# Layer 2's scan over both halves at once, with a prepared seam; drives made in pairs; thirteen of 32 states weighed on GpSimd

## The chip, the core and the metric

One core of a Trainium2 chip runs the whole program; the other cores are idle. The metric is the device time of one execution in microseconds (us). The kernel before took 38,971.14 us (median of three runs, 38,961.69 to 39,000.97).

## The reference, cut to what matters

Sixteen images of 64 x 64 pixels and 128 channels go through four layers, each of which normalises its input over the image and adds its result to it: linear attention, a Fourier layer, and two selective-scan layers (a cross scan in four directions over 256 channels with 16 states, then a plain one over 128 channels with 8 states). The change lies in the third of them, numbered 2. The reference's step of such a scan is, here in the form of layer 3:

```python
def step(h, inp):
    d_t, u_t, b_t, c_t = inp
    dA = jnp.exp(d_t[..., None] * A)
    h = dA * h + (d_t * u_t)[..., None] * b_t[:, None, :]
    y_t = jnp.einsum('bdn,bn->bd', h, c_t)
    return (h, y_t)
```

d_t is a softplus, dA the decay, d_t * u_t * b_t the drive, and the product with c_t the weighing.

## The kernel before

The outer loop takes one image after another. Layer 2's 256 channels stand as two halves of 128 partitions side by side, 512 pixels each, so a tile is 128 x 1024. A unit is one state of one chunk of 512 pixels: 4 directions x 8 chunks x 16 states make 512 units an image. g counts chunks over all directions, c chunks in a direction, n states, k directions; from k = 2 on the scan runs backwards. For each unit u:

- SyncE copies the rows of B and C to all partitions by DMA, two states at a time, four buffers deep (spread_rows, line 423).
- GpSimd multiplies du = softplus x input by the row of B into one of six tiles Q: make_drive (line 543, instruction at line 550), three units ahead.
- ScalarE writes the decays of the two halves to PSUM, one exponential for each (decays, line 1202), one unit ahead. The banks alternate between even and odd units.
- VectorE scans each half with tensor_tensor_scan (states, line 1585, instruction at line 1598). The first chunk starts from 0.0, later ones from the column that the chunk before left in HST2.
- ScalarE's carry (line 1219) copies the last column of the scan to HST2. It comes after the decays of u+1 in ScalarE's queue.
- The product with the row of C is made by VectorE (weigh, line 1606) or, for six of the 16 states, by GpSimd (weigh, line 554, instruction at line 561), which waits for the carry, since it overwrites the tile that the carry reads.
- TensorE adds the product up over the states with an identity matrix, and after the 16th VectorE takes the sum to SBUF (take_y, line 1568).

Each engine works through its queue in order, and the loops over u in the scan2 of each engine write this order out by hand. Between the units, chunk g+1 is prepared: TensorE's rows2 and steps2 (lines 830 and 839), ScalarE's split2 and softplus2 (1157 and 1165), VectorE's log_small2 (1556), then GpSimd's sum_dt (528) for each half and make_du (535). All ScalarE instructions are issued at line 1050, all matmuls but the transposes at line 668.

Layer 3 does the same with one half, 8 states and 64 units (block3 of each engine; project, variance and project_out at lines 981 to 994; VectorE's take_y, fuse and add at 1683, 1705 and 1715). At the end of an image SyncE stores it, loads the next (lines 497 to 506), waits for the four engines, clears every semaphore of the image (line 509) and lets them go on (meet, line 514). VectorE then takes the statistics of the new image (line 1448).

## Time and profile before

| | us |
|---|---|
| median of three runs | 38,971.14 |
| the profiled execution's own time | 38,973.72 |
| its span, first to last instruction | 38,971.8 |
| TensorE busy | 28,928.2 (74%) |
| VectorE busy | 33,856.0 (87%) |
| ScalarE busy | 20,211.0 (52%) |
| GpSimd busy | 30,997.3 (80%) |
| image one: layers 0 and 1, and layer 2 up to its scan | 0 to 331 |
| image one: scan of layer 2 | 331 to 2130 |
| image one: rest of layer 2, and layer 3 | 2130 to 2454 |

PE is TensorE's matmuls, PEld its weight loads, DVE VectorE, ACT ScalarE, POOL GpSimd and SPq SyncE's queue. In a row of a timeline stand the start in us, the duration in us, engine, line, operation, what is written and read, and the number of instructions merged; in brackets the idle time of the engine just before, and who ended it. PS is PSUM, WORK, XN and BIG are SBUF regions (Q, DT and half of the C rows lie in WORK, the B rows in XN). Instructions that follow each other closely overlap by some hundredths of a microsecond, so the distance from start to start is a little less than the duration.

### The profile page before, as it was taken

The page shows a single profiled execution, that of the slowest core. Times are in us where ns is not written, and L with a number is a line of the kernel's source. Part 1 is how long each engine was busy: PE and PEld are TensorE (multiplying, and loading weights), DVE is VectorE, ACT ScalarE, POOL GpSimd, SP SyncE. Part 2 cuts the span into 40 slices and gives each one's busy share as a digit, 9 for nine tenths or more (in the row PEclk, how much of TensorE's full clock was granted, in tenths as well). Part 3 has the DMA queues.
Part 4 walks back from the last instruction along what each step waited for, and adds up shares of the span by engine and source line. Part 5 has one row for each costly group of instructions (what it writes and reads, how often), then busy time and mean ns, then how long its engine had stood idle before and what let it go on. Part 6 is the DMA issues. An engine that isn't in the chain of part 4 may idle for free. (4 is left out here: it accounts for less than half of the span.)

```text
span 38971.8 us, 271091 instructions
## 1 busy us (share of the span) xinstructions
PE 28928.2 (74%) x61540; PEld 11465.7 (29%) x61540; DVE 33856.0 (87%) x33741; ACT 20211.0 (52%) x38037; POOL 30997.3 (80%) x14776
## 2 busy tenths in 40 slices
PE   7777777777777777777777777777777777777777
PEld 3232232322323223232232322323223232232322
DVE  8979889798897988979889798897988979889798
ACT  4545545455454554545545455454554545545455
POOL 6949869498694986949869498694986949869497
PEclk8898888988888888898888988888898898888988
DMA  3424334243342433424334243342433424334243
GB/s 114 151 95 151 137 111 151 96 152 135 112 151 96 152 134 111 151 96 151 136 112 151 95 152 134 111 151 95 152 136 112 152 96 152 134 113 151 96 152 134
DMA packets 1387318, 5029.11 MB, mean 129 GB/s; under 512 B 164272, under 2 KB 165816, under 8 KB 1381440
## 3 DMA queue, kind: packets, MB, share of 16 engines
q1 hardware_dynamic: 1385536, 5010.20, 37.0%
q8 instruction: 526, 8.62, 0.1%
q14 instruction: 1256, 10.29, 0.1%
HBM read 4938.25 MB, written 71.30 MB: 129 GB/s over the span
## 5 line engine op out<-in xcount | busy, mean ns | idle before, releaser
L668 PE MATMUL PS<-WORK,CST 128*128 128x512 f32 x36096 | 19719.3, 690 | 8147.0 <-POOL WORK L561 7315.7
L550 POOL TENSOR_TENSOR WORK<-WORK,XN 128x1024 f32<-128x1024 f32 x8192 | 19311.4, 2395 | 324.6 <-ACT BIG L1050 324.6
L668 PEld LDWEIGHTS PS<-WORK,CST 128*128 128x128 f32 x36096 | 7495.5, 219 | 20640.2 <-POOL WORK L561 10104.7
L1050 ACT ACTIVATE PS<-WORK,AN 128x512 f32<-128x512 f32 x17408 | 11306.4, 679 | 1828.1 <-DVE WORK L1606 1024.8
L1598 DVE TENSOR_TENSOR_SCAN PS<-PS,HST,WORK 128x512 f32<-128x512 f32 x8960 | 10971.9, 1271 | 29.7 <-ACT PS L1050 16.1
L1598 DVE TENSOR_TENSOR_SCAN WORK<-PS,HST,WORK 128x512 f32<-128x512 f32 x5376 | 6583.5, 1267 | 0.0
L561 POOL TENSOR_TENSOR WORK<-WORK,CWIDE 128x1024 f32<-128x1024 f32 x2048 | 4888.4, 2387 | 117.4 <-issue 59.7
L1050 ACT ACTIVATE HST<-PS 128x2 f32<-128x2 f32 x5152 | 859.0, 167 | 6498.6 <-DVE WORK L1606 6063.0
L1606 DVE TENSOR_TENSOR WORK<-PS,WORK 128x1024 f32<-128x1024 f32 x3072 | 3762.1, 1225 | 105.1
L638 POOL MEMSET XN<- 128x66 f32 x32 | 4.9, 154 | 4158.8 <-DVE SM L1452 4036.2
L1050 ACT ACTIVATE WORK<-PS,DTB 128x512 f32<-128x512 f32 x2304 | 1555.8, 675 | 2103.9 <-DVE WORK L1563 1669.6
L1050 ACT ACTIVATE WORK<-PS 40x512 f32<-40x512 f32 (+2 forms) x1600 | 933.8, 598 | 3163.2 <-PE PS L668 2859.3
L1606 DVE TENSOR_TENSOR WORK<-PS,CWIDE 128x1024 f32<-128x1024 f32 x2048 | 2508.3, 1225 | 69.9
L561 POOL TENSOR_TENSOR WORK<-WORK 128x1024 f32<-128x1024 f32 x1024 | 2450.9, 2393 | 25.5 <-DVE WORK L1598 23.1
L668 PE MATMUL PS<-XN,TAP 128*128 128x512 f32 x4608 | 2058.9, 601 | 34.6 <-DVE XN L1468 34.6
L533 POOL TENSOR_TENSOR WORK<-WORK 128x512 f32<-128x512 f32 x1024 | 1338.6, 1307 | 808.2 <-DVE WORK L1563 808.2
L607 POOL TENSOR_TENSOR WORK<-WORK 128x512 f32<-128x512 f32 x1024 | 1276.4, 1271 | 836.7 <-DMA WORK<-xbc_rows 769.0
L668 PE MATMUL PS<-BIG,XP 128*40 128x512 f32 x2304 | 1667.8, 810 | 293.9 <-ACT BIG L1050 293.9
L1050 ACT ACTIVATE WORK<-WORK,VEC 128x512 f32<-128x512 f32 x2304 | 1631.3, 708 | 0.0
L1598 DVE TENSOR_TENSOR_SCAN PS<-PS,WORK 128x512 f32<-128x512 f32 x1280 | 1489.7, 1209 | 121.9 <-ACT PS L1050 121.9
L540 POOL TENSOR_TENSOR WORK<-WORK,BIG 128x1024 f32<-128x1024 f32 x512 | 1354.8, 2646 | 1.3
L668 PE MATMUL PS<-WORK,DTW 8*128 8x512 f32 x2304 | 1286.5, 639 | 0.0
(161 smaller groups left out, 24604.0 us busy)
## 6 DMA issues: line engine op xcount, KB each, us to landing
XN<-xbc_rows SPq DMA_DIRECT2D x4096, 512.0 KB, 3.7
WORK<-xbc_rows SPq DMA_DIRECT2D x2816, 512.0 KB, 4.3
CWIDE<-xbc_rows SPq DMA_DIRECT2D x2304, 512.0 KB, 4.2
BIG<-in_spec_dram SPq DMA_DIRECT2D x32, 2048.0 KB, 12.1
X<-in_x_dram SPq DMA_DIRECT2D x68, 512.0 KB, 4.7
xbc_rows<-WORK SPq DMA_DIRECT2D x512, 64.0 KB, 3.1
out_dram<-X SPq DMA_DIRECT2D x64, 512.0 KB, 5.1
xbc_rows<-WORK SPq DMA_DIRECT2D x128, 32.0 KB, 1.6
```

The lines of the kernel that those rows point to most:

```text
L533: nc.gpsimd.tensor_tensor(dt, dt, S.LE[:, ch(h)], ADD).then_inc(S.dt_made, 1)
L540: nc.gpsimd.tensor_tensor(S.like(S.DU[g % 2], g), S.like(S.DT[g % 2], g), S.cols(BIG1, g), MUL).then_inc(S.du_ready, 1)
L550: nc.gpsimd.tensor_tensor(S.both(S.Q[u % 6]), S.both(S.DU[u // SN % 2]), S.wide(S.BW, u).unsqueeze(1).to_broadcast([P, 2, NT]), MUL).then_ ...
L561: nc.gpsimd.tensor_tensor(q, q, S.wide(S.CW, u).unsqueeze(1).to_broadcast([P, 2, NT]), MUL).then_inc(S.weighed_pool, 1)
L607: nc.gpsimd.tensor_tensor(S.Q[u % 6], S.DU[u // SN3 % 2], S.wide(S.BW, u), MUL).then_inc(S.drive, 1)
L638: nc.gpsimd.memset(XN3[:, 0, :], 0.0).then_inc(frame_zero, 1)
L668: return nc.tensor.matmul(o, w, r, start=start, stop=stop)
L1050: return nc.scalar.activation(o, i, f, **k)
L1598: r = V.tensor_tensor_scan(o, a, b, HST2[:, 2 * n + h:2 * n + h + 1] if c else 0.0, MUL, ADD)
L1606: V.tensor_tensor(S.both(S.Q[u % 6]), PS[:, lo:lo + 2, :], S.wide(S.CW, u).unsqueeze(1).to_broadcast([P, 2, NT]), MUL).then_inc(S.weighed_ ...
```

## The change

- **Scan.** states makes one scan over 1024 columns, through two neighbouring PSUM banks. So that the second half does not go on from the first, ScalarE's prepare(g) overwrites one column of DT, at the seam, with 1e33: the decay there becomes 0. What the second half starts from is put in the drive: seam(u) adds HST2 x decay to that one column of Q, by a ScalarE instruction on one element per partition whose scale and bias are both read by pointer. prepare(g) first takes the true decays of that column for all 16 states (AT2). The first chunk of a direction has no seam.
- **ScalarE's queue** at unit u is: decays of u+1, a part of the preparation of a later chunk, seam of u+2, carry of u. seam(u+2) waits for the drive of u+2 and for the carry of the chunk before.
- **Drives.** GpSimd makes the drives of u+2 and u+3 in one instruction of 2048 columns, at even u; both semaphore counts come at its end. It waits for the sums up to unit u-3. Its weighing of u comes behind it.
- **Weighing.** Of 32 units in a row, thirteen are weighed on GpSimd: 1, 3, 6, 8, 11, 13, 17, 19, 22, 24, 26, 28, 30.
- **Softplus.** The sum of its two parts is made by TensorE in PSUM (sum_dt2) and copied out by ScalarE (copy_dt2) instead of by GpSimd. The rows and steps of a chunk are made one chunk earlier.
- **Layer 3.** The last chunk's project, variance and project_out go to banks 3 and 4 instead of 7 and 5 and are spread over the states of the last round; the loops end one round earlier.
- **Between images.** 33 semaphores of layers 0 and 1 are cleared by SyncE inside spread_rows (i = 16), 39 of layer 2 inside spread_rows3 (i = 12). The statistics of the next image's first four chunks are taken before the engines meet.

The core of the diff:

```diff
@@ -24,7 +24,7 @@
 POOL_STATES3 = (2, 5)
-POOL_STATES = (1, 4, 6, 9, 12, 14)
+POOL_STATES = (1, 3, 6, 8, 11, 13, 17, 19, 22, 24, 26, 28, 30)
...
@@ -288,7 +302,7 @@
-                return u % SN in s.pool
+                return u % (2 * SN) in s.pool
...
@@ -311,6 +325,19 @@
+            def seam(s, k):
+                return (NT, 1) if k < 2 else (NT - 1, 0)
+            def long(s, u):
+                lo = s.banks(u)[0]
+                return PS[:, lo:lo + 2, :].rearrange("p b l -> p (b l)")
+            def prepares(s, g):
+                return sum(2 if v % NCH else 1 for v in range(g + 1))
...
@@ -318,6 +345,11 @@
+            def two(s, u):
+                at = 2 * NT * (u % 6)
+                return WORK[:, at:at + 4 * NT].rearrange("p (n d l) -> p n d l", n=2, d=2)
...
@@ -438,6 +470,9 @@
                             e.wait_ge(S.rows_stored, 16 * (i // 8 + 1))
+                        if i == 16:
+                            for t in past_layer1:
+                                e.sem_clear(t)
                         if i >= 4:
...
@@ -467,6 +512,9 @@
                             e.wait_ge(S.rows_stored, 16 * (i // 4 + 1))
+                        if i == 12:
+                            for t in past_layer2:
+                                e.sem_clear(t)
                         if i >= 4:
...
@@ -497,7 +546,8 @@
-                    e.sem_clear(x_loaded[i])
+                    if i >= 2:
+                        e.sem_clear(x_loaded[i])
...
@@ -505,10 +555,11 @@
                 e.wait_ge(sample_done, 4)
-                for s in persistent + [sample_done]:
-                    e.sem_clear(s)
+                for s in persistent + x_loaded[0:2] + [sample_done]:
+                    if s not in past_layer1 and s not in past_layer2:
+                        e.sem_clear(s)
                 e.sem_inc(next_sample, 1)
-            for i in range(4):
+            for i in (2, 3):
                 e.wait_ge(x_loaded[i], 16)
...
@@ -518,19 +569,14 @@
+            nc.gpsimd.memset(LIM[:, 0:1], 1e33).then_inc(lim_set, 1)
+            nc.gpsimd.memset(LIM[:, 1:2], -1e-30).then_inc(lim_set, 1)
...
-                def sum_dt(g, h):
-                    e.wait_ge(S.dt_steps, 4 * g + 2 * h + 2)
-                    e.wait_ge(S.softplus, 12 * g + 6 * h + 6)
-                    dt = S.DT[g % 2][:, ch(h)]
-                    nc.gpsimd.tensor_tensor(dt, dt, S.LE[:, ch(h)], ADD).then_inc(S.dt_made, 1)
...
@@ -540,16 +586,16 @@
-                def make_drive(u):
+                def make_drives(u):
...
-                        e.wait_ge(S.summed, u - 5)
-                    nc.gpsimd.tensor_tensor(S.both(S.Q[u % 6]), S.both(S.DU[u // SN % 2]),
-                                            S.wide(S.BW, u).unsqueeze(1).to_broadcast([P, 2, NT]),
-                                            MUL).then_inc(S.drive, 1)
+                        e.wait_ge(S.summed, u - 4)
+                    rows = S.BW[u // 2 % 4].rearrange("p (n l) -> p n l", n=2)
+                    nc.gpsimd.tensor_tensor(S.two(u), S.both(S.DU[u // SN % 2]).unsqueeze(1).to_broadcast([P, 2, 2, NT]),
+                                            rows.unsqueeze(2).to_broadcast([P, 2, 2, NT]), MUL).then_inc(S.drive, 2)
...
@@ -561,23 +607,15 @@
-                sum_dt(0, 0)
-                sum_dt(0, 1)
...
-                for u in range(3):
-                    make_drive(u)
+                make_drives(0)
...
-                    if g + 1 < KDIR * NCH:
-                        if n == 8:
-                            sum_dt(g + 1, 0)
-                        if n == 11:
-                            sum_dt(g + 1, 1)
-                        if n == 12:
-                            make_du(g + 1)
-                    if u + 3 < S.units:
-                        make_drive(u + 3)
+                    if g + 1 < KDIR * NCH and n == 12:
+                        make_du(g + 1)
+                    if u % 2 == 0 and u + 2 < S.units:
+                        make_drives(u + 2)
...
@@ -829,26 +867,35 @@
-                if h == 0 and g:
-                    e.wait_ge(S2.dt_steps, 4 * g)
+                if g:
+                    e.wait_ge(S2.dt_made, 2 * g - 1)
...
-                o = S2.like(bank(6), g)[0:40, 0]
+                o = S2.like(bank(7), g)[0:40, 0]
...
+                if g:
+                    e.wait_ge(S2.dt_made, 2 * g)
...
+            def sum_dt2(g, h):
+                e.wait_ge(S2.softplus, 12 * g + 6 * h + 6)
+                e.wait_ge(S2.dt_steps, 4 * g + 2 * h + 2)
+                mm(bank(7 - h), EYE, S2.DT[g % 2][:, ch(h)], True, False)
+                mm(bank(7 - h), EYE, S2.LE[:, ch(h)], False, True).then_inc(S2.dt_summed, 1)
...
-                        e.wait_ge(S.dt_steps, 4 * KDIR * NCH)
+                        e.wait_ge(S.dt_made, 2 * KDIR * NCH)
...
@@ -857,12 +904,19 @@
-                        if n < 2:
-                            rows2(g + 1, n)
-                        if n in (3, 4):
-                            steps2(g + 1, n - 3)
+                        if n == 5:
+                            sum_dt2(g + 1, 0)
+                        if n == 8:
+                            sum_dt2(g + 1, 1)
...
+                    if g + 2 < KDIR * NCH:
+                        if n == 9:
+                            for h in range(2):
+                                rows2(g + 2, h)
+                        if n == 12:
+                            for h in range(2):
+                                steps2(g + 2, h)
...
@@ -895,6 +949,17 @@
+                    if j == 4:
+                        for h in range(2):
+                            sum_dt2(0, h)
+                    if j == 5:
+                        e.wait_ge(conv_act, 2)
+                        e.wait_ge(dw_act, 2)
+                        for h in range(2):
+                            rows2(1, h)
+                    if j == 6:
+                        for h in range(2):
+                            steps2(1, h)
...
@@ -981,20 +1046,24 @@
-                    if j >= 1:
+                    if j == NCH - 1:
+                        e.wait_ge(c3_act, NCH)
+                    elif j >= 1:
...
-                    mm(bank(7), WO3[:, :], Y3[:, ch(j)]).then_inc(t_proj, 1)
+                    mm(S.out_bank(j), WO3[:, :], Y3[:, ch(j)]).then_inc(t_proj, 1)
...
-                    mm(bank(5), cst["ones"], S.SQ[j % 2]).then_inc(t_var, 1)
+                    if j == NCH - 1:
+                        e.wait_ge(u3_act, NCH)
+                    mm(S.var_bank(j), cst["ones"], S.SQ[j % 2]).then_inc(t_var, 1)
...
-                    mm(bank(7), WOUT3[:, :], Y3[:, ch(j)]).then_inc(g3_out, 1)
+                    mm(S.out_bank(j), WOUT3[:, :], Y3[:, ch(j)]).then_inc(g3_out, 1)
...
@@ -1004,9 +1073,17 @@
-                for c in range(-3, NCH + 2):
+                for c in range(-3, NCH + 1):
...
+                        if c == NCH:
+                            if n == 3:
+                                project(NCH - 1)
+                                project_out(NCH - 2)
+                            if n == 5:
+                                variance(NCH - 1)
+                            if n == 7:
+                                project_out(NCH - 1)
...
@@ -1185,8 +1262,13 @@
-                        e.wait_ge(S2.dt_made, 2 * g)
+                        e.wait_ge(S2.dt_summed, 2 * g + h - 1)
...
+            def copy_dt2(g, h):
+                e.wait_ge(S2.dt_summed, 2 * g + h + 1)
+                act(S2.DT[g % 2][:, ch(h)], bank(7 - h), ACT.Copy).then_inc(S2.dt_made, 1)
...
@@ -1199,11 +1281,36 @@
+                def prepare(g):
+                    k, c = g // NCH, g % NCH
+                    col, h = S.seam(k)
+                    step = S.DT[g % 2][:, col:col + 1]
+                    e.wait_ge(S.du_ready, g + 1)
+                    if c:
+                        at = (2 * k + h) * SN
+                        act(AT2[:, SN * (g % 2):SN * (g % 2 + 1)], AN2[:, at:at + SN], ACT.Exp,
+                            scale=step).then_inc(S.prepared, 1)
+                        e.wait_ge(S.prepared, S.prepares(g) - 1)
+                    act(step, LIM[:, 0:1], ACT.Copy).then_inc(S.prepared, 1)
+                def seam(u):
+                    k, c, n = S.of(u)
+                    g = u // SN
+                    col, h = S.seam(k)
+                    b = S.Q[u % 6][:, col:col + 1]
+                    e.wait_ge(S.drive, u + 1)
+                    e.wait_ge(S.carried, S.carried_by(u - SN))
+                    e.wait_ge(S.prepared, S.prepares(g) - 1)
+                    act(b, HST2[:, 2 * n + h:2 * n + h + 1], ACT.Identity,
+                        scale=AT2[:, SN * (g % 2) + n:SN * (g % 2) + n + 1], bias=b).then_inc(S.seamed, 1)
...
-                        e.wait_ge(S.dt_made, 2 * (u // SN) + 2)
+                        e.wait_ge(S.prepared, S.prepares(u // SN))
...
@@ -1229,18 +1336,31 @@
+                prepare(0)
...
+                softplus2(1, 0, 0)
...
-                        if n == 2:
-                            split2(g + 1)
-                        if 4 <= n < 10:
-                            softplus2(g + 1, (n - 4) // 3, (n - 4) % 3)
+                        if n in (0, 2):
+                            softplus2(g + 1, 0, 1 + n // 2)
+                        if n in (4, 5, 7):
+                            softplus2(g + 1, 1, (n - 3) // 2)
+                        if n in (9, 10):
+                            copy_dt2(g + 1, n - 9)
+                        if n == 14:
+                            prepare(g + 1)
...
+                    if g + 2 < KDIR * NCH:
+                        if n == 12:
+                            split2(g + 2)
+                        if n == 15:
+                            softplus2(g + 2, 0, 0)
+                    if u + 2 < S.units and S.of(u + 2)[1]:
+                        seam(u + 2)
...
@@ -1269,6 +1389,11 @@
                                 softplus2(0, h, part)
+                    if j == 4:
+                        for h in range(2):
+                            copy_dt2(0, h)
+                    if j == 5:
+                        split2(1)
                 exp_and_log()
...
@@ -1443,7 +1574,7 @@
                 if layer == 0:
-                    for j in range(NCH):
+                    for j in range(NCH // 2, NCH):
                         e.wait_ge(x_loaded[j // 2], 16)
...
@@ -1586,17 +1717,15 @@
+                    e.wait_ge(S.decay, 2 * u + 2)
...
-                    q = S.Q[u % 6]
-                    for h in range(2):
-                        e.wait_ge(S.decay, 2 * u + h + 1)
-                        a, b = bank(S.banks(u)[h]), q[:, ch(h)]
-                        o = b if S.on_pool(u) else a
-                        if k >= 2:
-                            a, b, o = a[:, ::-1], b[:, ::-1], o[:, ::-1]
-                        r = V.tensor_tensor_scan(o, a, b, HST2[:, 2 * n + h:2 * n + h + 1] if c else 0.0, MUL, ADD)
-                    r.then_inc(S.scanned, 1)
+                        e.wait_ge(S.seamed, S.carried_by(u - SN))
+                    a, b, first = S.long(u), S.Q[u % 6], 2 * n
+                    o = b if S.on_pool(u) else a
+                    if k >= 2:
+                        a, b, o, first = a[:, ::-1], b[:, ::-1], o[:, ::-1], 2 * n + 1
+                    V.tensor_tensor_scan(o, a, b, HST2[:, first:first + 1] if c else 0.0, MUL, ADD).then_inc(S.scanned, 1)
...
@@ -1614,9 +1743,9 @@
-                        if n == 7:
+                        if n == 3:
...
-                        if n == 10:
+                        if n == 8:
...
@@ -1752,12 +1883,19 @@
+            e.wait_ge(first_loaded, 32)
+            for j in range(NCH // 2):
+                V.bn_stats(GST[:, 6 * j:6 * j + 6], X[:, ch(j)])
...
+                for j in range(NCH // 2):
+                    e.wait_ge(x_loaded[j // 2], 16)
+                    r = V.bn_stats(GST[:, 6 * j:6 * j + 6], X[:, ch(j)])
+                link(r)
```

## Rows read from the trace of the kernel before

**Rows 1.** The page's busy times; then a stretch of image one.
```profile
PE 28928.2 (74%) x61540; PEld 11465.7 (29%) x61540; DVE 33856.0 (87%) x33741; ACT 20211.0 (52%) x38037; POOL 30997.3 (80%) x14776
...
331.00:2130.00 1799.00, 1294.94 (x2339) 463.83 (x2337) 1736.00 (x1570) 977.86 (x1897) 1782.43 (x797) 0.88 0.43 149
```

**Rows 2.** Timeline, GpSimd, one chunk of layer 2's scan (start, us, engine, line).
```profile
420.82 1.30 POOL L533 TENSOR_TENSOR WORK<-WORK 128x512 f32<-128x512 f32 x1
422.04 4.70 POOL L550 TENSOR_TENSOR WORK<-WORK,XN 128x1024 f32<-128x1024 f32 x2
426.65 2.39 POOL L561 TENSOR_TENSOR WORK<-WORK 128x1024 f32<-128x1024 f32 x1
428.96 2.40 POOL L550 TENSOR_TENSOR WORK<-WORK,XN 128x1024 f32<-128x1024 f32 x1
```

**Rows 3.** The same, VectorE.
```profile
433.49 2.45 DVE L1598 TENSOR_TENSOR_SCAN WORK<-PS,HST,WORK 128x512 f32<-128x512 f32 x2
...
452.51 1.41 DVE L1575 SCALAR_TENSOR_TENSOR BIG<-BIG,VEC,PS 128x512 f32<-128x512 f32 x2 [0.97 <-PE PS L668]
...
467.08 2.45 DVE L1598 TENSOR_TENSOR_SCAN WORK<-PS,HST,WORK 128x512 f32<-128x512 f32 x2
469.45 2.44 DVE L1598 TENSOR_TENSOR_SCAN PS<-PS,HST,WORK 128x512 f32<-128x512 f32 x2
471.93 1.23 DVE L1606 TENSOR_TENSOR WORK<-PS,CWIDE 128x1024 f32<-128x1024 f32 x1
473.07 0.69 DVE L1560 SCALAR_TENSOR_TENSOR PS<-PS,WORK 128x512 f32<-128x512 f32 x1
...
474.42 2.45 DVE L1598 TENSOR_TENSOR_SCAN PS<-PS,HST,WORK 128x512 f32<-128x512 f32 x2
```

**Rows 4.** Instruction groups by shape, images one and two (busy, mean ns).
```profile
L1598 DVE TENSOR_TENSOR_SCAN PS<-PS,HST,WORK 128x512 f32<-128x512 f32 x1120 | 1371.4, 1270 | 3.7 <-ACT PS L1050 2.0 <-POOL WORK L550 1.7
...
L1606 DVE TENSOR_TENSOR WORK<-PS,CWIDE 128x1024 f32<-128x1024 f32 x256 | 313.5, 1225 | 8.7
...
L540 POOL TENSOR_TENSOR WORK<-WORK,BIG 128x1024 f32<-128x1024 f32 x64 | 169.2, 2644 | 0.2
...
L1598 DVE TENSOR_TENSOR_SCAN PS<-PS,WORK 128x512 f32<-128x512 f32 x160 | 186.2, 1210 | 15.2 <-ACT PS L1050 15.2
...
L1050 ACT ACTIVATE BIG<-PS 128x512 f32<-128x512 f32 x80 | 44.5, 597 | 53.7 <-PE PS L668 49.1 <-PE PS L710 4.5
...
L1703 DVE TENSOR_TENSOR WORK<-PS,CWIDE 128x512 f32<-128x512 f32 x48 | 33.2, 692 | 7.4 <-DMA CWIDE<-xbc_rows 6.0
...
L1050 ACT ACTIVATE BIG<-PS,SM 128x512 f32<-128x512 f32 x32 | 21.3, 671 | 8.8 <-PE PS L668 8.8
```

**Rows 5.** Timeline, ScalarE, layer 2's scan.
```profile
420.36 0.15 ACT L1050 ACTIVATE HST<-PS 128x2 f32<-128x2 f32 x1
420.60 1.30 ACT L1050 ACTIVATE PS<-WORK,AN 128x512 f32<-128x512 f32 x2
421.84 0.67 ACT L1050 ACTIVATE WORK<-PS,DTB 128x512 f32<-128x512 f32 x1
...
435.98 0.21 ACT L1050 ACTIVATE HST<-WORK 128x2 f32<-128x2 f32 x1 [0.80 <-DVE WORK L1598]
...
1024.03 0.19 ACT L1050 ACTIVATE HST<-WORK 128x2 f32<-128x2 f32 x1
```

**Rows 6.** Timeline, GpSimd, the weighing behind that last carry.
```profile
1024.35 2.35 POOL L561 TENSOR_TENSOR WORK<-WORK,CWIDE 128x1024 f32<-128x1024 f32 x1 [0.31 <-issue]
```

**Rows 7.** Timeline, all engines, end of the first image.
```profile
2441.80 0.69 DVE L1718 TENSOR_TENSOR X<-X,PS 128x512 f32<-128x512 f32 x1 [2.17 <-PE PS L668]
...
2453.30 0.69 DVE L1718 TENSOR_TENSOR X<-X,PS 128x512 f32<-128x512 f32 x1 [2.17 <-PE PS L668]
...
2457.07 0.35 SPq L506 DMA_DIRECT2D X<-in_x_dram  x1
...
2469.75 4.84 DVE L1448 BATCH_NORM_STATS2 GST<-X 128x6 f32<-128x512 f32 x8 [15.76 <-issue]
```

More of the change, by code:

```diff
@@ L233, in carries, with out_bank, var_bank @@
                 return u < (NCH - 1) * SN3
+            def out_bank(s, j):
+                return bank(3 if j == NCH - 1 else 7)
+            def var_bank(s, j):
+                return bank(4 if j == NCH - 1 else 5)
             def wide(s, bufs, u):
@@ L365, in program @@
         weights_in = sem("weights_in"); zeroed = sem("zeroed"); vec_setup = sem("vec_setup")
-        act_setup = sem("act_setup"); pe_setup = sem("pe_setup"); vec_ready = sem("vec_ready")
+        lim_set = sem("lim_set"); act_setup = sem("act_setup"); pe_setup = sem("pe_setup"); vec_ready = sem("vec_ready")
         sample_done = sem("sample_done"); next_sample = sem("next_sample")
-        x_loaded = [sem(f"x_loaded{i}") for i in range(4)]; spec_loaded = sample_sem("spec_loaded")
+        first_loaded = sem("first_loaded"); x_loaded = [sem(f"x_loaded{i}") for i in range(4)]; spec_loaded = sample_sem("spec_loaded")
         x_stored = [sample_sem(f"x_stored{i}") for i in range(4)]
@@ L450, in spread_rows @@
                         load(S.CW, S.c_loaded, i - 1, SN)
+            past_layer1 = [k_proj, k_copied, k_max, k_shift, k_exp, qv_proj, v_copied, q_shifted, q_exp, q_norm, kT_made,
+                           kT_copied, qT_made, qT_copied, ctx_made, ctx_masked, m2_made, m2_ready, f_trans, f_transc,
+                           f_spec, f_specn, f_specp, f_mix, f_mixc, f_mixT, f_mixTc, f_inv, f_sum, h_proj, h_reluA,
+                           h_reluV, spec_loaded]
+            past_layer2 = [S2.rows_ready, S2.rows_copied, S2.rows_stored, S2.dt_raw, S2.softplus, S2.dt_steps, S2.dt_made,
+                           S2.dt_summed, S2.prepared, S2.seamed,
+                           S2.du_ready, S2.decay, S2.drive, S2.scanned, S2.carried, S2.weighed_dve, S2.weighed_pool,
+                           S2.summed, S2.y_taken, *S2.b_loaded, *S2.c_loaded, conv_done, conv_act, px_made, px_copied,
+                           dw_done, dw_act, y_mean, y_cent, y_sq, y_var, y_rstd, y_norm]
             def spread_rows3(e):
@@ L1025, in block3 @@
                             project_z(c + 1)
-                        if n == 6 and S.has(c - 2):
+                        if n == 6 and S.has(c - 2) and c < NCH:
                             project_out(c - 2)
@@ L1162, in split2 @@
                     e.wait_ge(S2.rows_stored, 16 * g)
-                act(S2.R[0:40, :], bank(6)[0:40, :], ACT.Copy).then_inc(S2.rows_copied, 1)
+                act(S2.R[0:40, :], bank(7)[0:40, :], ACT.Copy).then_inc(S2.rows_copied, 1)
             def softplus2(g, h, part):
@@ L1364, in square @@
                         e.wait_ge(t_var, base + j - 1)
-                    act(S.SQ[j % 2], bank(7), ACT.Square).then_inc(t_sq, 1)
+                    act(S.SQ[j % 2], S.out_bank(j), ACT.Square).then_inc(t_sq, 1)
                 def rstd(j):
@@ L1370, in rstd @@
                     e.wait_ge(t_rstd, base + j)
-                    link(act(S.LV, bank(5), ACT.Ln, bias=vec["eps"]))
+                    link(act(S.LV, S.var_bank(j), ACT.Ln, bias=vec["eps"]))
                     if j >= 2:
@@ L1390, in silus @@
                     exp_and_log()
-                for c in range(-2, NCH + 2):
+                for c in range(-2, NCH + 1):
                     for n in range(SN3):
                         u = SN3 * c + n
+                        if c == NCH:
+                            if n == 4:
+                                square(NCH - 1)
+                            if n == 5:
+                                rstd(NCH - 1)
                         if 0 <= u + 1 < S.units:
@@ L1707, in fuse @@
                     e.wait_ge(t_rstd, base + j + 1)
-                    t = bank(7)
+                    t = S.out_bank(j)
                     V.tensor_tensor(t, t, S.RS[j % 2], MUL).then_inc(t_norm, 1)
@@ L1717, in add @@
                     e.wait_ge(g3_out, j + 1)
-                    V.tensor_tensor(X[:, ch(j)], X[:, ch(j)], bank(7), ADD).then_inc(x_added, 1)
-                for c in range(-1, NCH + 2):
+                    V.tensor_tensor(X[:, ch(j)], X[:, ch(j)], S.out_bank(j), ADD).then_inc(x_added, 1)
+                for c in range(-1, NCH + 1):
                     for n in range(SN3):
@@ L1734, in block3 @@
                             add(c - 2)
+                fuse(NCH - 1)
+                add(NCH - 1)
             e.wait_ge(weights_in, NLOADS)
```

12 lines of the change are left out of this document (9 added, 3 removed).

## The prediction

> **What bounds the kernel now.** I read the page's busy shares first: GpSimd and VectorE are both near full over the whole span [rows 1]. The table of stretches then places that: from 331 to 2130 us of the first image, the scan of layer 2, GpSimd is busy 1782 of 1799 us and VectorE 1736 [rows 1]. That stretch is 32 chunks (four directions of eight), so a chunk takes 1799 / 32 = 56.2 us, and 16 images spend 28,784 of 38,971.8 us there. Next come the timelines of one chunk: GpSimd's instructions start one behind the other, 2.31 us per 1024 columns and 1.22 us per 512 [rows 2]. Its work in a chunk is 16 drives and 6 weighings at 2.31, two sums at 1.22 and one make_du at 2.57 (mean of 2.64 less the 0.07 that neighbours overlap) [rows 2, 4]: 55.8 us. So GpSimd is the bound; VectorE is right behind and idles about 1 us a chunk, before take_y [rows 3].
>
> **What the change takes off these two.** GpSimd: a drive of 2048 columns. Two points give its slope, 1.09 us per 512 columns, so 2.31 + 2 x 1.09 = 4.49 us against 4.62 for two [rows 2]. Bounds: 4.34 if the fixed part goes wholly, 4.62 if grouping saves nothing; I take 4.49, the straight line. The sums (2.44 a chunk) leave for TensorE and ScalarE; half a weighing more comes. Work per chunk: 8 x 4.49 + 6.5 x 2.31 + 2.57 = 53.5 us.
>
> VectorE: today a pair of scans takes 2.37 us (result in SBUF) or 2.48 (in PSUM), a weighing 1.14, the softplus pair 1.35 [rows 3]. No row shows a scan of 1024 columns. It saves at least nothing, at most about 0.2: the fixed part of an elementwise instruction is 0.16 busy (692 ns at 512 columns, 1225 at 1024) and the start value by pointer 0.06 (1270 against 1210) [rows 4]; of the first, about half overlaps the neighbour. I take 0.12. A unit weighed on GpSimd costs VectorE 2.25, another 3.50, a chunk 6.5 x 2.25 + 9.5 x 3.50 + 2.7 + about 2 for take_y = 52.6 us. ScalarE gets two copies, 16 seams and the prepares, some 6 us beside 30; TensorE four matmul calls on 512 columns. Both engines have room in the sum (72% and 54% busy in that stretch [rows 1]), so this work itself costs nothing; if VectorE waited for it, take_y would be late first.
>
> **What it adds: a closed chain.** Before, GpSimd made the drive of unit u+3, then weighed u. Now it makes u+2 and u+3 together at even u, then weighs u or u+1. ScalarE's queue at unit u is now: exponentials of u+1, seam of u+2, carry of u. The seam of u+2 waits for the drive just being made; the carry stands behind it; GpSimd's weighing of u waits for that carry. So behind every pair of drives GpSimd stops until ScalarE has answered, however far VectorE is.
>
> - Even unit: signal to ScalarE 0.04 (the nearest row is VectorE's: scan ended 435.94, carry began 435.98) [rows 3, 5], seam 0.26, carry 0.20, signal to GpSimd 0.13 (1024.22 to 1024.35) [rows 5, 6]: 0.63.
> - Odd unit: the drive came at u-1, and ScalarE first answers that unit's queue: signal 0.04, seam 0.26, carry of u-1 0.24, then two exponentials 1.24, seam 0.26, carry 0.20, signal 0.13: 2.37 [rows 5, 6].
>
> A seam is not in the trace. It is a carry (0.19) with two operands read by pointer, each of which costs 0.07 (597 to 671 ns) [rows 4, 5]: 0.35 busy, 0.26 to the next start. Bounds: 0.10 (a plain carry's distance) and 0.35.
>
> Each wait also loses the 0.07 of overlap: 0.70 and 2.44. Of the thirteen units weighed on GpSimd in 32, seven are even and six odd: 7 x 0.70 + 6 x 2.44 = 19.5 us per two chunks. The work is 107.0. Unit 17 adds 1.1: no weighing precedes it, so GpSimd is ready for it 4.49 + 2.37 = 6.9 us after drives 16/17, but scan 16 can start only 1.9 after them (seam, carry, exponentials), and 3.50 + 2.25 + 0.37 for carry and signals make 8.0. Sum: 127.6, that is **63.8 us a chunk against 56.2**.
>
> This holds in six of eight chunks of a direction. The last has no carry and the first no seam, so GpSimd waits for scans only. Stepping both queues through them with the same durations gives 56.3 and 57.4: GpSimd is only two units ahead now, and after unit 11 its weighing, make_du and two drives (9.2 us) outlast VectorE's 5.75 us of work. I take 57. A direction: 6 x 63.8 + 2 x 57 = 497 against 449.8, so +47 us, and 64 directions +3,000 us.
>
> VectorE needs 52.6 us a chunk, so a dearer scan (2.37) would alter only unit 17's wait: under 100 us in all.
>
> The Trainium skill (Perfetto Trace Analysis, Optimizing Scalar/DVE Operations) has a rule on each side: grouping into larger operations helps a saturated engine, while an engine that isn't saturated but causes bubbles on others may do better with its instructions broken up. By the first alone the time would be the faster rival below; this trace shows GpSimd saturated but has no run with bubbles from grouping.
>
> **Outside the scan.** The last project in layer 3 no longer waits for the bank of the sixth: today the two adds are 11.5 us apart (2441.80, 2453.30) [rows 7]; what remains on that path is the norm of the last chunk itself, and I take 3.5 us saved of at most 5. Between images VectorE waits from 2453.99 to 2469.75. The last load is issued at 2457.07, and 134 semaphores are cleared before 2469.7: 12.3 / 134 = 0.092 us each [rows 7]. 72 are now cleared earlier and five are new, so 67 x 0.092 = 6.2 us go; four of eight statistics (2.4 us of 4.84) move ahead of the meeting. That makes 8.6. Against it, 39 clears (3.6 us) stand in SyncE's queue ahead of chunk 3's row loads in layer 3: 0 to 3.6, mostly covered by loads already issued. The 33 in layer 2 stand behind four buffers of lead and cost nothing, unless rows come late. The earlier start of chunk 1's steps in block2 puts a wait for VectorE ahead of three convolutions of TensorE, -2 to +2. Together -11 an image: -180.
>
> **Sum.** Against the profiled execution's 38,973.7 us (span 38,971.8, median of the runs 38,971.1, so no correction): 38,973.7 + 3,000 - 180 = 41,790 us.
>
> **Rivals.**
> 1. *Faster.* The waits of GpSimd hide behind VectorE, so that only the sums of work count: GpSimd 53.5, VectorE 52.6, with the stall at make_du about 54.5 a chunk. 512 x -1.7 - 180 gives 37,920 us. For it: both engines do lose work. Against: the chain above never passes VectorE; GpSimd alone releases it. It decides if GpSimd's idle time stays under 56.2 - 53.5 = 2.7 us a chunk; I find 10.3 in six of eight. Chance 0.06. That the idle time comes out at about those 2.7 us, and so no change: 0.03.
> 2. *Dear drives.* The drive's pattern has one more level. make_du, which walks columns the other way in half of its calls, means 2.64 against 2.39 busy [rows 2, 4]. If the pair paid that rate, 0.25 per 1024, it would be 0.5 x 8 x 512 = +2,000: 43,800. Against: its inner run is still 512 neighbours. Chance 0.05.
> 3. *The change's scan saves nothing* (two banks cost as two scans). On this path it alters next to nothing, within the forecast's range; it would matter only in rival 1, which then ends at 38,600.
>
> **Numbers.** Forecast 0.86, rivals 0.06, 0.03 and 0.05. Range: drives at 4.34 or 4.62 are -600 or +530; a seam at 0.10 or 0.35 takes 7 x 0.16 + 6 x 0.32 = 3.0 per two chunks off or adds 1.7, over 384 chunks -590 or +320. So 40,600 to 42,640, opened at the lower end for waits that VectorE's lag may cover in part: 40,200 to 42,700. Measurement can tell 0.2% (78 us) from no change: faster by more 0.06, within 0.03, slower 0.91.
>
> **What the profile would show.** Drives 4.5 us long, 128 x 2048. GpSimd idle about 9 to 10 us a chunk in the middle chunks, ahead of its weighings, released by ScalarE: some 0.65 before even, 2.4 before odd. ScalarE idle at its seams, released by GpSimd. VectorE near 85% busy in the scan. Scans near 2.35 us. The next image's statistics about 10 us after the last add. Wrong would be: GpSimd gapless (rival 1), drives over 5 us (rival 2), or odd and even waits alike, which would mean that the exponentials are not in the chain.

## The result, and the profile after

The changed kernel takes **42,243.9 us** (median of 4 runs, 42,223.33 to 42,246.12) against 38,966.42 us (median of 4, 38,958.89 to 39,000.97) for the kernel before, measured beside it: ratio 1.0837, 95% interval 1.0820 to 1.0854. It is slower, by 3,278 us. The forecast was 41,790 us with a range of 40,200 to 42,700: right in sign, cause and range, 454 us (1.1%) too low. The profiled execution took 42,246.12 us, with a span of 42,244.3. One execution of run 6's kernel (69,625.56 us at a granted clock of 0.465) and one of the kernel before beside run 9 (49,360.38 us at 0.641) were slow ones and enter no ratio.

The page's busy times after the change, then the scan of layer 2 in the first image (columns as in [rows 1]):

```profile
PE 31061.1 (74%) x65636; PEld 12611.9 (30%) x65636; DVE 32925.0 (78%) x25297; ACT 22829.5 (54%) x47189; POOL 29855.2 (71%) x9914
```
```profile
329.00:2340.00 2011.00, 1423.13 (x2589) 534.59 (x2587) 1678.00 (x1042) 1140.35 (x2466) 1713.68 (x496) 0.86 0.39 134
```

Against [rows 1], GpSimd and VectorE both have less work over the span (29,855 for 30,997 us, 32,925 for 33,856), and yet the span is longer. The stretch says where: 2011 us for 1799. GpSimd is busy 1713.68 / 32 = 53.6 us a chunk, the 53.5 of the prediction, and idle (2011 - 1713.7) / 32 = 9.3 us a chunk, where it was idle 0.5. VectorE is busy 1678 / 32 = 52.4, forecast 52.6. The forecast saving of work is there; the idle time is new.

GpSimd's timeline in one chunk (columns as in [rows 2]):

```profile
450.21 2.34 POOL L607 TENSOR_TENSOR WORK<-WORK,CWIDE 128x1024 f32<-128x1024 f32 x1 [0.65 <-issue]
452.51 4.51 POOL L597 TENSOR_TENSOR WORK<-WORK,XN 128x2048 f32<-128x2048 f32 x1
457.67 2.35 POOL L607 TENSOR_TENSOR WORK<-WORK,CWIDE 128x1024 f32<-128x1024 f32 x1 [0.65 <-issue]
459.98 4.53 POOL L597 TENSOR_TENSOR WORK<-WORK,XN 128x2048 f32<-128x2048 f32 x1
466.91 2.36 POOL L607 TENSOR_TENSOR WORK<-WORK 128x1024 f32<-128x1024 f32 x1 [2.41 <-issue]
469.22 4.52 POOL L597 TENSOR_TENSOR WORK<-WORK,XN 128x2048 f32<-128x2048 f32 x1
476.15 2.35 POOL L607 TENSOR_TENSOR WORK<-WORK 128x1024 f32<-128x1024 f32 x1 [2.41 <-issue]
...
518.87 8.98 POOL L597 TENSOR_TENSOR WORK<-WORK,XN 128x2048 f32<-128x2048 f32 x2
531.81 2.36 POOL L607 TENSOR_TENSOR WORK<-WORK 128x1024 f32<-128x1024 f32 x1 [3.96 <-DVE WORK L1728]
```

L597 are the pairs of drives, L607 the weighings. Behind each pair GpSimd stops for 0.65 us before an even unit and 2.41 before an odd one, the same to the hundredth where one pair stands between two weighings, which fits an answer that hangs on the pair itself. Behind two pairs in a row it is 0.88 (units 6 and 22). The last line is unit 17. The trace puts about half of this waiting down to "issue" and the rest to VectorE or TensorE, at the same lengths. Who answers is in ScalarE's timeline of the same moment (columns as in [rows 5]):

```profile
464.54 0.39 ACT L1127 ACTIVATE WORK<-HST,WORK,AT 128x1 f32<-128x1 f32 x1 [1.53 <-POOL WORK L597]
464.83 0.15 ACT L1127 ACTIVATE HST<-PS 128x2 f32<-128x2 f32 x1
465.08 1.30 ACT L1127 ACTIVATE PS<-WORK,AN 128x512 f32<-128x512 f32 x2
466.32 0.37 ACT L1127 ACTIVATE WORK<-HST,WORK,AT 128x1 f32<-128x1 f32 x1
466.59 0.19 ACT L1127 ACTIVATE HST<-WORK 128x2 f32<-128x2 f32 x1
```

The first is a seam, released by the pair that began at 459.98; then the carry of unit u-1, the two exponentials, the second seam, the carry of u (here unit 1 of a chunk) at 466.59, and GpSimd weighs at 466.91. That is the chain of the prediction, link by link. Over the whole execution, ScalarE's waits and the groups by shape (total, times, longest; and as in [rows 4]):

```profile
ACT WORK L1127 <- POOL WORK L597: 11313.8, 2960, 9.3
...
DVE PS L1728 <- ACT PS L1127: 2911.9, 1624, 17.3
```
```profile
L597 POOL TENSOR_TENSOR WORK<-WORK,XN 128x2048 f32<-128x2048 f32 x4096 | 18483.0, 4521 | 284.3 <-ACT BIG L1127 251.0 <-PE PS L706 32.5
L607 POOL TENSOR_TENSOR WORK<-WORK 128x1024 f32<-128x1024 f32 x2048 | 4821.7, 2354 | 3512.9 <-DVE WORK L1728 1744.8 <-issue 1268.7 <-PE PS L706 371.1
L607 POOL TENSOR_TENSOR WORK<-WORK,CWIDE 128x1024 f32<-128x1024 f32 x1280 | 3007.5, 2350 | 1083.8 <-issue 927.3 <-PE PS L706 127.3 <-DVE WORK L1728 29.1
```
```profile
L1127 ACT ACTIVATE WORK<-HST,WORK,AT 128x1 f32<-128x1 f32 x7168 | 2712.3, 378 | 11313.8 <-POOL WORK L597 11313.8
```
```profile
L1728 DVE TENSOR_TENSOR_SCAN PS<-PS,HST,WORK 128x1024 f32<-128x1024 f32 x4224 | 9924.3, 2350 | 2769.7 <-ACT PS L1127 2634.6 <-ACT WORK L1127 96.1 <-issue 22.7
```

ScalarE waits 11,314 us at its seams, all of it for the pair of drives, and GpSimd 3512.9 + 1083.8 = 4,597 us at its weighings: 9.0 us in each of 512 chunks. VectorE's scans in turn wait for exponentials that stand behind those seams.

### The profile page after: what moved, and what is told of

It reads as the page before. It is cut to its first block and busy times, and to the rows that moved or that the text cites. A ratio compares the mean times of both kernels' runs of the same rounds, so it can differ in the third digit from the quotient of the medians.

```text
span 42244.3 us, 286554 instructions
## 1 busy us (share of the span) xinstructions
PE 31061.1 (74%) x65636; PEld 12611.9 (30%) x65636; DVE 32925.0 (78%) x25297; ACT 22829.5 (54%) x47189; POOL 29855.2 (71%) x9914
## 5 line engine op out<-in xcount | busy, mean ns | idle before, releaser
L706 PE MATMUL PS<-WORK,CST 128*128 128x512 f32 x40192 | 22023.3, 697 | 9376.5 <-POOL WORK L607 6664.0
L597 POOL TENSOR_TENSOR WORK<-WORK,XN 128x2048 f32<-128x2048 f32 x4096 | 18483.0, 4521 | 284.3 <-ACT BIG L1127 251.0
L1728 DVE TENSOR_TENSOR_SCAN PS<-PS,HST,WORK 128x1024 f32<-128x1024 f32 x4224 | 9924.3, 2350 | 2769.7 <-ACT PS L1127 2634.6
L1127 ACT ACTIVATE WORK<-HST,WORK,AT 128x1 f32<-128x1 f32 x7168 | 2712.3, 378 | 11313.8 <-POOL WORK L597 11313.8
L1728 DVE TENSOR_TENSOR_SCAN WORK<-PS,HST,WORK 128x1024 f32<-128x1024 f32 x2944 | 6900.4, 2344 | 1813.5 <-ACT PS L1127 1803.0
L607 POOL TENSOR_TENSOR WORK<-WORK 128x1024 f32<-128x1024 f32 x2048 | 4821.7, 2354 | 3512.9 <-DVE WORK L1728 1744.8
L607 POOL TENSOR_TENSOR WORK<-WORK,CWIDE 128x1024 f32<-128x1024 f32 x1280 | 3007.5, 2350 | 1083.8 <-issue 927.3
L1728 DVE TENSOR_TENSOR_SCAN PS<-PS,WORK 128x1024 f32<-128x1024 f32 x640 | 1462.8, 2286 | 546.0 <-ACT PS L1127 277.3
L645 POOL TENSOR_TENSOR WORK<-WORK 128x512 f32<-128x512 f32 x1024 | 1275.1, 1269 | 839.9 <-DMA WORK<-xbc_rows 774.3
L1127 ACT ACTIVATE WORK<-PS 128x512 f32<-128x512 f32 (+2 forms) x2624 | 1514.9, 586 | 591.9 <-PE PS L706 303.1
```

The costliest lines, as they stand in the source:

```text
L597: nc.gpsimd.tensor_tensor(S.two(u), S.both(S.DU[u // SN % 2]).unsqueeze(1).to_broadcast([P, 2, 2, NT]), rows.unsqueeze(2).to_broadcast([P, ...
L607: nc.gpsimd.tensor_tensor(q, q, S.wide(S.CW, u).unsqueeze(1).to_broadcast([P, 2, NT]), MUL).then_inc(S.weighed_pool, 1)
L645: nc.gpsimd.tensor_tensor(S.Q[u % 6], S.DU[u // SN3 % 2], S.wide(S.BW, u), MUL).then_inc(S.drive, 1)
L706: return nc.tensor.matmul(o, w, r, start=start, stop=stop)
L1127: return nc.scalar.activation(o, i, f, **k)
L1728: V.tensor_tensor_scan(o, a, b, HST2[:, first:first + 1] if c else 0.0, MUL, ADD).then_inc(S.scanned, 1)
```

## The experiments

Each is one edit of the changed kernel unless it says otherwise. Runs 1 to 4 are one execution each, beside one of the kernel before (38,984.9 us); for the others the median of several is given, beside 38,979.1 us for the kernel before in runs 5 to 8.

**1. The carry ahead of the seam.** Same instructions, other order in ScalarE's queue at unit u:

```
+                    if S.of(u)[1] < NCH - 1:
+                        carry(u)
                     if u + 2 < S.units and S.of(u + 2)[1]:
                         seam(u + 2)
-                    if S.of(u)[1] < NCH - 1:
-                        carry(u)
```

> Only ScalarE's queue is changed: at unit u the carry of u stands ahead of the seam of u+2. Theory A (the waits of GpSimd are the chain drive, seam, carry, weighing): the wait of 0.65 us before each even weighing goes; the one of 2.41 before each odd weighing falls to 0.04 + 0.29 + 1.24 + 0.20 + 0.13 = 1.9, since the seam of the even unit and the exponentials still stand ahead of that carry. Two middle chunks fall from 127.8 to about 120 us, the time by 384 x 3.9 = 1,500 to about 40,750. Theory B (a lead of only two units for the drives is what costs, whatever ScalarE does between): the order in ScalarE's queue changes nothing, 42,100 to 42,300.

Measured 40,911.57 us: 1,332 us less than the changed kernel, and 162 above the expected 40,750. GpSimd's timeline:

```profile
452.97 2.37 POOL L607 TENSOR_TENSOR WORK<-WORK,CWIDE 128x1024 f32<-128x1024 f32 x1
455.28 4.54 POOL L597 TENSOR_TENSOR WORK<-WORK,XN 128x2048 f32<-128x2048 f32 x1
461.69 2.35 POOL L607 TENSOR_TENSOR WORK<-WORK 128x1024 f32<-128x1024 f32 x1 [1.87 <-issue]
```

The even wait is gone, the odd one is down to 1.87: the carry no longer stands behind a seam, but the exponentials still do. Two neighbours were swapped and nothing else, so for these 1,332 us the order is at fault, not the work.

**2. The seam one unit ahead instead of two.** `seam(u + 2)` becomes `seam(u + 1)`, still ahead of the carry.

> Only ScalarE's queue is changed: at unit u it makes the seam of u+1 instead of that of u+2. Theory A: an even weighing no longer waits for a drive, an odd one waits 0.04 + 0.29 + 0.20 + 0.13 = 0.65 behind its seam, with no exponentials between. Two middle chunks: work 106.9 + 6 x 0.72 + about 1.4 at unit 17 = 112.7 us, so 42,244 - 384 x 7.5 = about 39,350. Theory B: unchanged, 42,100 to 42,300.

Measured 39,373.67 us, expected 39,350. Now the exponentials are out of the chain as well, and the odd wait is the even one of before:

```profile
454.09 4.54 POOL L597 TENSOR_TENSOR WORK<-WORK,XN 128x2048 f32<-128x2048 f32 x1
459.27 2.36 POOL L607 TENSOR_TENSOR WORK<-WORK 128x1024 f32<-128x1024 f32 x1 [0.65 <-issue]
```

The weighing of unit 11 waits 1.63 us here, for VectorE's scan, which the expectation did not have. Two middle chunks take 114.2 us for the expected 112.7, and the chunks at the ends of a direction make up for it: that the total agrees to 24 us is in part luck.

**3. No seams at all.** This kernel leaves out a part of the work: the second half of every chunk but the first of a direction starts from its drive alone.

> Leaves out the seams (the second half of a chunk starts from its drive alone). Pairs of drives, the single scan and all else stay. Theory A: no instruction of ScalarE waits for a drive; GpSimd waits for scans alone, and every middle chunk takes what the first chunk of a direction takes, 56.5 to 57.5 us: 42,244 - 384 x 7 = about 39,550. Theory B: GpSimd still loses some 10 us a chunk, 42,000 or more.

Measured 39,034.65 us, lower than expected by 515. Behind the pairs that waited before there is now almost no gap; what is left stands at units 11 and 17 (2.19 and 2.07 us), and there GpSimd waits for VectorE's scan:

```profile
452.69 4.53 POOL L597 TENSOR_TENSOR WORK<-WORK,XN 128x2048 f32<-128x2048 f32 x1
457.17 2.37 POOL L607 TENSOR_TENSOR WORK<-WORK 128x1024 f32<-128x1024 f32 x1
...
491.16 2.35 POOL L607 TENSOR_TENSOR WORK<-WORK 128x1024 f32<-128x1024 f32 x1 [2.19 <-DVE WORK L1725]
```

With its waits the seam costs some 3,200 us. As work alone it is 0.29 us sixteen times a chunk, on an engine that is half idle, and run 5 keeps all of it in a kernel that is faster than before. But this kernel, without any seam, is still no faster than before, though GpSimd has 2.3 us a chunk less to do (53.5 for 55.8). The waits for scans point at the short lead of two units, which the next run changes together with the pair.

**4 and 5. Single drives, three units ahead.** The pair is split again, and everything else of the change stays, seams two ahead included:

```
-                    if u % 2 == 0 and u + 2 < S.units:
-                        make_drives(u + 2)
+                    if u + 3 < S.units:
+                        make_drive(u + 3)
```

> Single drives three units ahead, as in the kernel before; seams, the single scan, the sums on TensorE, thirteen of 32 and all else as in the changed kernel. Theory A: the seam of u+2 finds its drive made one unit earlier, so GpSimd has no wait for ScalarE: 16 x 2.31 + 6.5 x 2.31 + 2.57 = 54.6 us a chunk, 512 x 8.1 = 4,150 less than 42,244: about 38,100, faster than the kernel before. ScalarE's added load as the cause (theory C) would leave the time above 40,000 with ScalarE's queue late; the load is the same here.

> The same edit as in the run with single drives three units ahead (one look gave 38,462.0 us, 1.3% under the kernel before), now timed in rounds. If the closed chain through the pair of drives is the whole loss, this kernel, with the long scan, the seam, the softplus sums on TensorE and the part outside the scan all kept, stays faster than before: ratio 0.985 to 0.989. Rival: that one look was luck, and the ratio is within 0.2% of 1.

The two runs are the same kernel. The single execution of run 4 took 38,462.0 us, and the four of run 5 have a median of 38,470.0 (38,454.87 to 38,487.7; 38,979.1 before), ratio 0.987, interval 0.9856 to 0.9884. The seams of unit u+2 now find a drive that was made a unit earlier, the chain is open, and GpSimd runs nearly without gaps:

```profile
453.35 6.98 POOL L596 TENSOR_TENSOR WORK<-WORK,XN 128x1024 f32<-128x1024 f32 x3
460.29 2.35 POOL L607 TENSOR_TENSOR WORK<-WORK 128x1024 f32<-128x1024 f32 x1
462.59 4.66 POOL L596 TENSOR_TENSOR WORK<-WORK,XN 128x1024 f32<-128x1024 f32 x2
467.22 2.34 POOL L607 TENSOR_TENSOR WORK<-WORK 128x1024 f32<-128x1024 f32 x1
```

The whole loss of the change, and 500 us more, hangs on the pair and its lead of two. Both were changed at once: no run has pairs with a longer lead, or single drives with a lead of two, so what each alone costs is not shown. The time is 360 us above the expected 38,100, though GpSimd is busy 792 of 800 us. The middle chunks take 55.1 us for the 54.6 of its work alone, and each image loses 8.5 us at the start of layer 2, of which more below.

**6. The same, with 12 of 32 states on GpSimd**, the six of 16 of the kernel before:

```
-POOL_STATES = (1, 3, 6, 8, 11, 13, 17, 19, 22, 24, 26, 28, 30)
+POOL_STATES = (1, 4, 6, 9, 12, 14, 17, 20, 22, 25, 28, 30)
```

> Single drives three units ahead, and GpSimd weighs 12 of 32 states instead of 13. One weighing of 2.31 us per two chunks leaves GpSimd: 1.16 x 512 = 590 us less if GpSimd alone sets the time, 37,870. VectorE takes 1.25 for it per two chunks and would need about 53.5 us a chunk, GpSimd 53.4, so the two meet: 38,050 expected. Rival: VectorE (or its wait for make_du) already sets the time, and 38,350 to 38,700 comes out.

**37,988.32 us**, ratio 0.9744, interval 0.9732 to 0.9757: 2.6% faster than before and the fastest kernel here. The stretch from 500 to 1300 us of image one in the changed kernel, in run 4 and in this one:

```profile
500.00:1300.00 800.00, 561.85 (x1014) 209.41 (x1014) 667.94 (x419) 451.23 (x988) 679.77 (x197) 0.85 0.40 134
```
```profile
500.00:1300.00 800.00, 604.22 (x1155) 223.26 (x1154) 759.35 (x479) 524.55 (x1115) 792.49 (x342) 0.91 0.45 154
```
```profile
500.00:1300.00 800.00, 624.99 (x1183) 234.13 (x1182) 779.96 (x495) 535.53 (x1131) 789.91 (x340) 0.90 0.45 156
```

GpSimd (the last busy time) stays near 790 of 800 while VectorE rises from 759 to 780: the freed time was filled with more chunks. The thirteenth state cost 38,470 - 37,988 = 482 us, 0.94 a chunk, where half a weighing is 1.16.

**7. The pair kept, the seam one unit ahead, 12 of 32 states.**

> The changed kernel with the seam prepared one unit ahead instead of two (39,373.7 alone), and 12 of 32 states weighed on GpSimd. Chain theory: only the odd weighings (units 1 and 9) still wait, 0.65 each, and the long waits at units 11 and 17 go because two units without a weighing now precede them less often; work 8 x 4.49 + 6 x 2.31 + 2.57 = 52.4, with waits 53.8 a chunk: 38,000 to 38,200. Rival: waits of GpSimd for VectorE remain with a lead of two units however the states are spread, 38,800 to 39,200.

39,038.97 us (39,029.4 to 39,057.48), ratio 1.0016, interval 1.0007 to 1.0025: the rival, not my chain theory, which had left out two waits. GpSimd's timeline:

```profile
531.89 2.36 POOL L607 TENSOR_TENSOR WORK<-WORK,CWIDE 128x1024 f32<-128x1024 f32 x1
535.81 4.54 POOL L597 TENSOR_TENSOR WORK<-WORK,XN 128x2048 f32<-128x2048 f32 x1 [1.56 <-PE PS L706]
541.55 2.35 POOL L607 TENSOR_TENSOR WORK<-WORK 128x1024 f32<-128x1024 f32 x1 [1.20 <-DVE WORK L1728]
```

A pair needs two free buffers of the six at once: its first drive is held back until TensorE has freed the buffer of its second (1.56 here), where a single drive needs only its own; and with a lead of only two units the weighing behind it waits for its scan (1.20). Over the whole execution the pairs wait 568 us for TensorE and the weighings 1,447 us; in run 6 the single drives never wait for TensorE and the weighings 451 us. The pair with a lead of two is worse than singles with a lead of three even with the seam one unit later: 39,039 against 37,988 with the same states.

**8. The kernel before with only the edits outside layer 2's scan.** Layer 3's last chunk in other banks, clears moved, half of the statistics ahead of the meeting.

> The kernel before with only the edits outside the scan of layer 2: last chunk of layer 3 in other banks, clears moved into layers 2 and 3, half of the statistics ahead of the meeting. The prediction gave these 11 us an image, of them 2 for a cause not in this kernel: 38,970 - 180 = 38,790. The trace of the changed kernel reads 7.4 us an image: 38,850. Rival: a part of the gain is lost to late row loads behind the clears, 38,930 or more.

38,794.15 us (38,782.5 to 38,799.7), ratio 0.9952, interval 0.9939 to 0.9964: 185 us less than 38,979.1, or 11.6 an image; the prediction had 11. The 38,850 expected just before this run, from 7.4 us an image in the changed kernel's trace, was the worse guess: that figure held a loss at the start of layer 2, which is not in this kernel (see below). VectorE at the end of the first image:

```profile
2433.74 0.69 DVE L1762 TENSOR_TENSOR X<-X,PS 128x512 f32<-128x512 f32 x1 [1.22 <-PE PS L695]
...
2440.43 0.69 DVE L1762 TENSOR_TENSOR X<-X,PS 128x512 f32<-128x512 f32 x1 [2.17 <-PE PS L695]
2441.15 2.47 DVE L1812 BATCH_NORM_STATS2 GST<-X 128x6 f32<-128x512 f32 x4
2452.93 2.47 DVE L1492 BATCH_NORM_STATS2 GST<-X 128x6 f32<-128x512 f32 x4 [9.31 <-issue]
```

The last two adds are 6.7 us apart where [rows 7] had 11.5, and the second half of the statistics ends at 2455.40, 14.3 us after the last add; in [rows 7] that is 2469.75 + 4.84 = 2474.59, or 20.6 after it. 4.8 + 6.3 = 11.1 us.

**9. Two scans of 512 columns in the version of run 6**, and so neither seam nor prepared column; the softplus sums stay on TensorE.

> The version with single drives three ahead and 12 of 32 states on GpSimd (37,988.3 us), with two scans of 512 columns a unit as before, and so with no seam and no prepared column; the softplus sums stay on TensorE. If the long scan saves VectorE the 0.12 us a unit of the prediction, VectorE needs 1.9 us more a chunk, 54.0 against 52.1 in the trace of that version, and passes GpSimd's 53.4: with about 0.6 of its idle time, 54.6 a chunk, 38,600 us. Rival: the long scan saves nothing, its bank pair costing what two scans cost (the prediction's third rival), or GpSimd alone sets the time: within 0.3% of 37,988.

38,416.3 us (38,410.06 to 38,437.96), ratio 0.9861, interval 0.9843 to 0.9878. The long scan is worth 428 us there, so the rival falls, but less than the 610 expected. VectorE with two scans, and with one (run 6):

```profile
547.11 2.44 DVE L1725 TENSOR_TENSOR_SCAN WORK<-PS,HST,WORK 128x512 f32<-128x512 f32 x2
549.47 2.44 DVE L1725 TENSOR_TENSOR_SCAN PS<-PS,HST,WORK 128x512 f32<-128x512 f32 x2
551.94 1.23 DVE L1733 TENSOR_TENSOR WORK<-PS,WORK 128x1024 f32<-128x1024 f32 x1
```
```profile
545.14 2.34 DVE L1729 TENSOR_TENSOR_SCAN WORK<-PS,HST,WORK 128x1024 f32<-128x1024 f32 x1
547.40 2.33 DVE L1729 TENSOR_TENSOR_SCAN PS<-PS,HST,WORK 128x1024 f32<-128x1024 f32 x1
549.77 1.23 DVE L1736 TENSOR_TENSOR WORK<-PS,CWIDE 128x1024 f32<-128x1024 f32 x1
```

From start to start the pair takes 2.36 and 2.47 us, the long scan 2.26 and 2.37: 0.10 saved, 1.6 us a chunk. In the same stretch of 800 us VectorE is busy 790 and GpSimd 779 with two scans: the bound has passed to VectorE. That only 0.84 of the 1.6 us a chunk shows fits this change of bound, but no run tests it.

**The parts, chained through these kernels:** outside the scan -185 (run 8); the sums off GpSimd, with the other moves of their steps, -378 (run 8 to run 9: 38,794.2 to 38,416.3); the long scan with its seams -428 (9 to 6); the thirteenth state +482 (6 to 5); the pair of drives two units ahead +3,774 (5 to the changed kernel). Each is the difference of two neighbouring kernels, so their sum, +3,265, is bound to be the changed kernel's 42,243.9 less the first 38,979.1, and checks nothing. The kernel before took 38,956.5 us beside run 9, 22.6 less than beside runs 5 to 8, so the -378 and the -428 can each be off by some 20. The order matters too: each figure holds for the bound that its neighbours leave.

## Why the prediction was right, and where it was off

**What bounded the kernel, and the work taken off**: held. A pair of drives is 4.52 us busy; from its start to the next instruction's, where none waits, it is 4.48 (452.69 to 457.17, run 3) for a forecast 4.49. Grouping saves GpSimd 0.14 us of 4.62. Scan 2.35 busy as forecast, 0.10 saved for 0.12. GpSimd 53.6 and VectorE 52.4 busy a chunk for 53.5 and 52.6.

**The closed chain**: held, and run 1 and run 2 took it apart link by link. Waits 0.65 and 2.41 for forecast 0.63 and 2.37. The seam is 0.38 busy and 0.29 to the next start (464.54 to 464.83) for 0.35 and 0.26; the bounds of the latter were 0.10 and 0.35. Two middle chunks take 128.3 us (66.8 and 61.5, from first scan to first scan, mean over all images) for 127.6. The differences: unit 17 with 3.96 for the 1.1 + 2.37 = 3.5 of the forecast, the 0.88 at units 6 and 22 for 0.63, and 0.03 for each seam.

**Rival 1** (waits hidden, 37,920) needed GpSimd idle under 2.7 us a chunk; it was idle 9.3. That run 6 gives 37,988 is a coincidence of numbers: it has single drives and 12 states. The kernel nearest to the rival's sum, with thirteen states and the chain open, is run 5 with 38,470. The Trainium skill (Perfetto Trace Analysis, Optimizing Scalar/DVE Operations) states both rules for ScalarE and VectorE: that larger operations can help an engine that is saturated, and that breaking up instructions may help where these two aren't saturated but cause bubbles on other engines. For VectorE's scan the runs agree with the first: VectorE is busy 790 of 800 us in run 9, and the grouped scan gains 428 us. The drives are GpSimd's, of which the section does not speak. Carried over to them the first rule would have misled: GpSimd was near full before (1782 of 1799 us), and the pairs with their lead of two cost 3,774. **Rival 2** (dear drives) fell with 4,521 ns. Its price was an average too: make_du takes 2.40 us on average in directions 0 and 2 and 2.89 in 1 and 3 of the kernel before, so a call that walks the columns the other way costs about 0.5 more, not 0.25. **Rival 3** (scan saves nothing) fell in run 9.

**Where the 454 us went.** The range held, and the mechanism. Two terms were mis-sized; the figures that follow are means over the images of each trace.

*The start of layer 2*, which the sum took at 0 ("-2 to +2"), costs 8.5 us an image, or 135 us: from layer 2's normalisation to its first scan 92.5 us for 84.0. The prediction looked for a wait on VectorE there. What the trace shows is work. TensorE has no gap among its convolutions of that stretch, neither before nor after, and the change puts the softplus sums of chunk 0 and the rows and steps of chunk 1 between them. Before, and after, on TensorE:

```profile
296.07 38.90 PE L668 MATMUL PS<-XN,TAP 128*128 128x512 f32 x90
```
```profile
306.45 3.60 PE L706 MATMUL PS<-WORK,CST 128*128 128x512 f32 x8
309.88 7.89 PE L706 MATMUL PS<-XN,TAP 128*128 128x512 f32 x18
317.70 1.91 PE L706 MATMUL PS<-BIG,XP 128*40 128x512 f32 x4
319.54 7.99 PE L706 MATMUL PS<-XN,TAP 128*128 128x512 f32 x18
327.47 1.98 PE L706 MATMUL PS<-WORK,DTW 8*128 8x512 f32 x4
329.38 7.99 PE L706 MATMUL PS<-XN,TAP 128*128 128x512 f32 x18
```

From start to start the three take 3.43 + 1.84 + 1.91 = 7.2 us. The forecast's "this work itself costs nothing" was taken from TensorE's 72% in the scan, and this stretch lies ahead of the scan. Run 9, which has the same moves but no prepared column, and whose scan waits only for its own half's exponentials, needs 91.9 us and run 8 without them 84.1: 7.7 of the 8.5 come with the moves, the rest with the column and the long scan. Which of the three moves costs how much was not run.

*The scan itself* grew from 1792.2 to 1999.8 us an image, first scan to last sum: 207.6 for the forecast 188, over 16 images 3,320 us for 3,000. The middle chunks are 2.3 us a direction above the forecast, the first and last of a direction 1.1 below (112.9 for 114). The larger part is the reference: the 449.8 us for a direction before was the whole stretch divided by four, with the wait for the first scan and the last sum in it, while 497 was stepped through the chunks alone; chunk to chunk a direction took 447.0 before and 498.0 after. The last chunk's end in each image adds 3.4.

*Outside layer 2's start and scan* the changed kernel gains 11.5 us an image for a forecast 11, and run 8 gains 11.7 there, so next to nothing of these edits is lost. The sum held; its parts did not. The last chunk gave 4.8 for 3.5, the meeting 6.3 for 8.6. Of the latter the statistics are 2.4, as forecast. The clears were dear in the prediction because 12.3 / 134 = 0.092 us spreads everything between the last load and the next image over them: in the changed kernel the same stretch takes 8.33 us with 67 clears (2665.00 to 2673.33), for 12.25 with 134. So a clear less saves 3.92 / 67 = 0.06 us, and some 4.4 us do not depend on the clears, an estimate from these two points.

## What to carry to other kernels

Before two operations of a producer are grouped, ask what the *second* engine's queue does behind the first thing that waits for them: a grouped producer delays its first result by its whole second half, leaves a shorter lead here (two units for three), and needs two buffers free at once. A tiny instruction (0.38 us) that waits for the newest result must not stand in an in-order queue ahead of one that the producer waits for; swapping two neighbours in that queue was worth 1,332 us here. And when both ends of a pipeline are near full, move work only until they meet: one state in 32 too many on the fuller engine cost 482 us. Room on an engine holds for the stretch in which it was read: TensorE had it in the scan, and none among the convolutions just ahead of it, where the same moves cost 7.7 us an image.

## What the runs showed of the hardware

Waits that are closed through two engines repeat to 0.01 us, chunk after chunk. The trace labels 2,196 of the 4,597 us of waits at the weighings "issue", although a chain through ScalarE makes them; others of the same length carry another engine's name. One scan of 1024 columns across two banks is busy 2,350 ns, two of 512 columns 2 x 1,270 = 2,540; from start to start the long one saves 0.10 us. The granted TensorE clock in the stretch from 500 to 1300 us was 0.85 in the changed kernel, where TensorE began the fewest matmuls (1,014), and 0.91 and 0.90 in runs 4 and 6 with 1,155 and 1,183. The order is not strict: 0.88 before with 1,035, and 0.87 in run 7 with 1,136. What sets the clock was not tested.
